# Two layers of attention and quantised feed-forward on one core: the passage from the first layer to the second put in another order

## The chip, the cores and the metric

One core of a Trainium2 chip runs the whole program once. The time is that of one execution on the device in microseconds; lower is better. Five instruction streams run side by side and wait for each other by semaphores: TensorE (PE), VectorE (DVE), ScalarE (ACT), GpSimd (POOL) and SyncE (SP, which here only issues transfers).

## What is computed

The input x is 8 batches of 256 rows of 512 values (16 row tiles of 128, `NT`; 8 batches, `NB`), with a context of 256 rows per batch. Two layers follow; each adds an attention and then a feed-forward part to x, both on a normalised x. Cut to what the change touches:

```python
# layer 0, feed-forward
h = square(relu(bitlinear(x, w1)))           # activations to 8 bits, weights to -1, 0, 1
x = x + bitlinear(h, w2)                     # "the way down"
# layer 1, cross-attention
Q = layernorm(x) @ W_qkv[:512].T             # projection
scores = coef * Q @ ctx.T                    # 256 scores for each row
thr = top_k(scores, 54)[-1]                  # the 54th largest
att = softmax(where(scores < thr, -inf, scores))
x = x + (att @ ctx) @ W_o.T                  # values, output projection
# layer 1, feed-forward
h = rms_norm(silu(bit_linear(x, w_gate)) * bit_linear(x, w_up), ln_weight)
x = x + bit_linear(h, w_down)
```

## The kernel before

Layer 0's attention, layer 0's feed-forward (`ffn0`) and layer 1 (`layer1`) are written one after another on every engine. Each part has a program per engine, a list of calls in an order written out by hand; there is no scheduler. A helper such as `pe_xb` is TensorE's share of a step, `act_qT` ScalarE's, and so on; each starts with the waits (`wait_ge`) that its inputs and its buffers need.

`ffn0` goes over the 16 row tiles. For tile n: transposes of the quantised row tile (`pe_x_turn`), the way up into the four banks of `quad` (`pe_up`, L1356), relu (L1453) and square (L1443) on ACT, rounding on DVE (`dve_hh`, L1578), transposes of the hidden values (`pe_h_turn`, L1370), their cast on ACT (`act_hT`, L1461), the way down (`pe_down`, L1381) and the residual on DVE (`dve_x2`, L1584), which SP stores to `x2_scratch`. Between these steps it also prepares layer 1's feed-forward weights in 48 chunks (`act_l`, L2575 and L2577, and the clip `dve_l`, L2582). The chunks 42 to 47 are finished in or after the passage to layer 1.

`layer1` handles a batch b (row tiles 2b and 2b+1) in stages s. In stage s batch s gets its projection and its scores, batch s-1 its weights, values and output projection, and the tiles of batch s-2 their feed-forward. The attention's matmuls run in float32 split in two parts (three products each, `PRODUCTS`), so each cast on ACT is followed by a subtraction on DVE or POOL that makes the lower part. The steps, by name and line:

- `pe_xa_turn` (L1779), `act_xT` (L2000), `dve_xT` (L2166): the normalised row tile is transposed and split. `dve_xa` (L2151 and three small ones) and `pool_xn` (L2401) make it.
- `pe_xb` (L1799), `act_qT` (L2006), `dve_qT` (L2172): projection, in two halves j of 24 matmuls.
- `act_ctx` and `pool_ctx` (L1990 and L1994 on ACT, L2390 on POOL): the context split for the scores (c = 0) and for the values (c = 1). `act_w`, `pool_w`: the same for the two attention weights.
- `pe_xc` (L1813), `act_sc` (L2014), `act_exp` (L2023): scores of a tile, 12 matmuls, their copy and exponential.
- `dve_top` (L2193) and six times `dve_round` (L2203, L2206): the search, 8 values of each row a round for both tiles of a batch. `dve_pm` (L2214) masks.
- `pe_xd` (L1828), `act_pT`, `dve_pT` (L2177): transposes of the attention weights.
- `pe_xe` (L1844), `act_oT`, `dve_oT` (L2183): values. `pe_xf` (L1859), `dve_x3` (L2188): output projection and residual.
- `dve_fa`, `pool_fn`, `dve_fq` (L2231), `act_xh` (L2038), `pe_x_turn` (L1877), `act_xq` (L2044): the tile normalised, quantised, transposed.
- `pe_gate_up` (L1892), `act_silu` (L2051), `dve_h` (L2247), `pool_hw` (L2433), `pe_h_turn`, `pe_down` (L1919), `dve_x4`: the feed-forward. Rounds of a search are put between the four `dve_h` of a tile.

PSUM has eight banks: `bA` (two), `bM`, `bT` and the four of `quad`. In layer 1 before the change the projection, scores, values and output projection use `bA[0]` and `bA[1]`, all float transposes `bT`, and only the feed-forward `quad`. `bA[1]` is also the bank of `ffn0`'s way down, so the second half of the first projection waits for the last residual:

```python
if b == 0:
    pe.wait_ge(f["w_lo"], 18)
    if j:
        pe.wait_ge(f["x2"], NT)
```

`pe_keep` issues matmuls on constants whose result nobody reads, ahead of a wait.

## Time and profile before

| | us |
|---|---|
| median of 3 runs | 1565.17 (1564.62 to 1567.32) |
| the profiled execution | 1567.12 |
| its span on the core | 1565.8 |
| TensorE busy | 1499.0 (96%) |
| VectorE busy | 1133.5 (72%) |
| ScalarE busy | 990.5 (63%) |
| GpSimd busy | 693.5 (44%) |

The span runs from the first to the last instruction; the execution's time has a little around it. Busy times are sums over instructions, and since matmuls overlap, a full TensorE need not be at its peak. The granted clock of TensorE over the span is 0.995 of full speed. Layer 0's attention lasts until about 870 us, its feed-forward until about 1195, and layer 1 has its regular turns from about 1265 on.

### The profile page before, as it was taken

Reading aid. Unit: us, or ns where it says so; the run is one execution under the profiler, and the core shown is the slowest. Engines: PE = TensorE matmul, PEld = TensorE weight load, DVE = VectorE, ACT = ScalarE, POOL = GpSimd, SP = SyncE. Lnnn points to the kernel's source line nnn. Section 1 sums busy time; section 2 is a strip of 40 time slices with the busy share of each in tenths; the row PEclk is TensorE's granted clock in tenths of the full one; section 3 lists DMA queues with packets and bytes.
Section 4 is the critical chain, followed back from the end, with each engine's and each line's share of the span. In section 5 each row is a group of like instructions: output and inputs, shape, how many; then the busy total and the mean of one; then the engine's idle time right before and its main releaser. Section 6 shows DMA issues by size and latency. Waiting matters only on the chain.

```text
span 1565.8 us, 26657 instructions
## 1 busy us (share of the span) xinstructions
PE 1499.0 (96%) x8840; PEld 1174.1 (75%) x8882; DVE 1133.5 (72%) x2966; ACT 990.5 (63%) x2502; POOL 693.5 (44%) x832
## 2 busy tenths in 40 slices
PE   7999999999999999999999899999996899999988
PEld 5778888888888888888887666666665666666653
DVE  7787777777777767777787745555556888888774
ACT  5666666666666666666677765666666576666655
POOL 5555555554555555555576200000005455555444
PEclk9999999999999999999999999999999899999999
DMA  7011111111111111111336666666655201111000
GB/s 277 28 54 55 41 68 41 48 62 41 49 61 41 60 46 40 60 47 48 122 124 265 242 243 215 219 220 220 222 183 190 80 21 55 55 48 41 28 14 28
DMA packets 50537, 156.73 MB, mean 100 GB/s; under 512 B 5600, under 2 KB 5728, under 8 KB 48992
## 3 DMA queue, kind: packets, MB, share of 16 engines
q1 hardware_dynamic: 50400, 155.02, 27.9%
q8 instruction: 72, 1.18, 0.3%
q14 instruction: 65, 0.53, 0.1%
HBM read 113.05 MB, written 41.94 MB: 99 GB/s over the span
## 4 chain that ended last, share of the span: by engine, by line
PE 75%; DVE 13%; ACT 5%; issue 3%; DMA 2%; POOL 2%; SPq 0%; ACTq 0%; DVEq 0%; POOLq 0%
PE bank L1327 11%; PE bank L368 10%; PE bank L421 9%; PE bank L338 8%; PE quad L408 5%; PE quad L1892 4%; PE bank L1381 3%; PE quad L1356 3%; PE bank L1919 3%; PE quad L396 3%; PE quad L398 3%; PE quad L397 3%; PE bank L1799 2%; PE bank L380 2%; PE bank L1859 1%
## 5 line engine op out<-in xcount | busy, mean ns | idle before, releaser
L617 ACT ACTIVATE Pt<-Pt,small 128x384 f32<-128x384 f32 (+1 forms) x256 | 172.8, 683 | 106.0 <-DVE small L877 105.9
L421 PE MATMUL bank<-PT,vv 128*128 128x512 f32 x672 | 200.2, 406 | 10.5 <-DVE PT L862 5.5
L368 PE MATMUL bank<-wq,xT 128*128 128x512 f32 x768 | 206.8, 404 | 1.3 <-DVE wq L772 0.8
L1137 POOL TENSOR_SCALAR Pt<-Pt,small 128x384 f32<-128x384 f32 (+1 forms) x256 | 164.7, 657 | 82.9 <-DVE small L885 82.8
L877 DVE CUSTOM_DVE_ANT_0 Pt<-quad,mask,small 128x384 f32<-128x384 f32 (+1 forms) x256 | 171.6, 679 | 33.8 <-PE quad L398 32.4
L1327 PE MATMUL bank<-wq,ot 128*128 128x512 f32 x768 | 189.2, 399 | 0.9 <-DVE xr L1513 0.8
L862 DVE TENSOR_TENSOR PT<-quad,PT 128x512 fp32r<-128x512 f32 x224 | 153.7, 686 | 38.5 <-ACT PT L609 38.1
L1327 PEld LDWEIGHTS bank<-wq,ot 128*128 128x128 f32 x768 | 142.7, 189 | 32.8 <-issue 1.2
L368 PEld LDWEIGHTS bank<-wq,xT 128*128 128x128 f32 x768 | 136.7, 188 | 26.9 <-DVE wq L772 2.1
L1125 POOL TENSOR_TENSOR t<-t 128x512 f32<-128x512 f32 x64 | 83.8, 1309 | 144.2 <-DVE t L843 144.2
L421 PEld LDWEIGHTS bank<-PT,vv 128*128 128x128 f32 x672 | 116.7, 189 | 34.8 <-DVE PT L862 12.8
L1630 POOL TENSOR_TENSOR cl<-cl,fixed 128x1 f32<-128x1 f32 x16 | 8.8, 551 | 297.8 <-DVE cl L1519 297.8
L609 ACT CAST PT<-quad 128x512 fp32r<-128x512 f32 x224 | 128.9, 591 | 7.0 <-PE quad L408 7.0
L408 PE MATMUL quad<-fixed,Pt 128*128 128x128 f32 x896 | 129.0, 272 | 0.9 <-POOL Pt L1137 0.9
L408 PEld LDWEIGHTS quad<-fixed,Pt 128*128 128x128 f32 x896 | 109.2, 140 | 24.4 <-POOL Pt L1137 2.2
L625 ACT CAST OT<-bank 128x512 fp32r<-128x512 f32 x64 | 37.6, 588 | 140.5 <-PE bank L421 140.5
L2433 POOL TENSOR_TENSOR bhw<-bh,lnw 128x512 f32<-128x512 f32 x64 | 81.7, 1276 | 82.8 <-DVE bh L2247 82.8
L396 PE MATMUL quad<-kT,qT 128*128 128x384 f32 (+1 forms) x256 | 99.4, 388 | 2.2 <-DVE small L877 0.8
L1131 POOL TENSOR_TENSOR small<-small,fixed 128x4 f32<-128x4 f32 x64 | 66.2, 1034 | 72.2 <-DVE small L849 72.1
L338 PE MATMUL bank<-wkc,cT 128*128 128x256 f32 x744 | 97.1, 287 | 0.6 <-issue 0.6
L338 PEld LDWEIGHTS bank<-wkc,cT 128*128 128x128 f32 x744 | 90.9, 191 | 8.2 <-DVE vv L828 7.0
L338 PE MATMUL bank<-wkv,xT 128*128 128x256 f32 x744 | 96.5, 286 | 0.0
(278 smaller groups left out, 3541.6 us busy)
## 6 DMA issues: line engine op xcount, KB each, us to landing
ot_scratch<-OT SPq DMA_DIRECT2D x64, 512.0 KB, 2.6
ot<-ot_scratch SPq DMA_DIRECT2D x64, 512.0 KB, 3.4
wkv_f<-in_w SPq DMA_DIRECT2D x12, 512.0 KB, 6.0
wkc_f<-in_w SPq DMA_DIRECT2D x12, 512.0 KB, 6.5
wkv_f<-in_wg SPq DMA_DIRECT2D x11, 512.0 KB, 4.3
wkv_f<-in_wd SPq DMA_DIRECT2D x11, 512.0 KB, 5.1
wkv_f<-in_wu SPq DMA_DIRECT2D x10, 512.0 KB, 4.9
stg<-in_ctxT SPq DMA_DIRECT2D x16, 256.0 KB, 3.5
```

The source lines that it names most:

```text
L338: ins = pe.matmul(kv_bank(u)[:, t * 256:t * 256 + 256], src[i][:, k, t * 128:t * 128 + 128], w[j][:, g, k, :], start=(n == 0), stop=(n == 11))
L368: ins = pe.matmul(bQ[:], xT[p][:, k, qt * 128:qt * 128 + 128], wq[j][:, g, k, :], start=(part == 0 and k == 0), stop=(part == 2 and k == 3))
L396: pe.matmul(bank[:, 0:n], qh, kh, start=True, stop=False)
L408: ins = pe.transpose(bP[k % 2][:, h * 128:h * 128 + 128], Pt[i % 2][:, h, kt * 128:kt * 128 + 128], idf[:])
L421: ins = pe.matmul(bO[:], vv[x][:, bg % 2, kt, :], PT[y][:, k % 2, :], start=(kt == 0 and n == 0), stop=(kt == tiles_in(i) - 1 and n == 2))
L609: act.copy(PT[0][:, k % 2, :], bP[k % 2]).then_inc(f["pt_hi"], 1)
L617: act.activation(p, p, ACT.Exp, bias=nm[:, i % 2, h:h + 1], scale=-1.0, accum_out=sm[:, i % 2, h:h + 1]).then_inc(f["s_exp"], 1)
L862: dve.tensor_tensor(PT[1][:, k % 2, :], bP[k % 2], PT[0][:, k % 2, :].bitcast(F32), ALU.subtract).then_inc(f["pt_lo"], 1)
L877: dve.tensor_tensor_reduce(Pt[i % 2][:, h, 0:n], bS[h % 2][:, 0:n], mask[:, 512 - n:512], scale=cq[:, i % 2, h:h + 1], scalar=3.0e38, op0= ...
L1125: pool.tensor_tensor(t1[:], t1[:], t2[:], ALU.add).then_inc(f["q_add"], 1)
L1137: pool.tensor_scalar(p, p, ri[:, i % 2, h:h + 1], 1.0, ALU.mult, ALU.mult).then_inc(f["p_n"], 1)
L1327: ins = pe.matmul(bY[:], ot[:, c % 4, i, k * 128:k * 128 + 128].bitcast(F32R), wo[j][:, g, k, :], start=(g == 0 and k == 0 and q == 0), st ...
```

## The change

The passage from `ffn0` to `layer1` is written in another order on every engine; what is computed stays the same, apart from `pe_keep` matmuls (5, 4 and 8 new ones; the 17 write banks that nobody reads at that time).

- Banks: new helpers choose the bank by batch or tile. The second half of batch 0's projection goes to `quad` bank 0, the scores of tiles 1, 2 and 3 to `quad` banks 0 and 1, the transposes of tiles 2 to 5 to `quad` banks 2 and 3.
- TensorE: `ffn0` ends its last tile with `pe_first`. There batch 0's projection is done in one piece, its scores come behind the transposes of the hidden values, and the last way down comes behind the scores and the transposes of batch 1. Batch 1's projection and scores follow. Stage 1 then goes from weights and values straight to the output projection, with the transposes of tiles 4 and 5 between.
- ACT and DVE: `act_first`, `dve_first` and `dve_second` write out stage 0 and stage 1 for these engines. The chunks 42 to 44 come behind batch 1's projection on ACT, 45 to 47 behind the first casts for batch 2. The last residual (`dve_x2`) stands behind the first round of batch 0's search. Batch 1's search has four rounds ahead of the first `dve_h`, before three.
- POOL: batch 1's context parts come ahead of the output weights. SP: three loads of context come earlier, ahead of the last store and the norm weights.

```diff
+    def q_bank(b, j):
+        return quad[:, 0, :] if (b, j) == (0, 1) else bA[j][:]
+
+    def s_bank(n):
+        return quad[:, n % 2, :] if n in (1, 2, 3) else bA[n % 2][:]
+
+    def x_bank(n):
+        return quad[:, 2 + n % 2, :] if 2 <= n < 6 else bT[:]
...
             if j:
-                pe.wait_ge(f["x2"], NT)
+                pe.wait_ge(f["relu"], 6 * (NT - 1) + 1)
         if b == 1:
             pe.wait_ge(f["sc"], j + 1)
+            if j:
+                pe.wait_ge(f["x2"], NT)
...
+    def pe_first():
+        pe_xb(0, 0)
+        pe_xb(0, 1)
+        ffn["pe_h_turn"](NT - 1)
+        pe_xc(0)
+        pe_xc(1)
+        pe_xa_turn(2)
+        pe_xa_turn(3)
+        ffn["pe_down"](NT - 1)
+        pe_xb(1, 0)
+        pe_xb(1, 1)
+        mem["pe_keep"](bM[:], 5)
+        pe_xc(2)
+        pe_xc(3)
+        mem["pe_keep"](bM[:], 4)
...
             if n == NT - 1:
-                l1["act_qT"](0, 0)
+                l1["act_ctx"](0, 0)
...
+    def act_first():
+        act_xT(2)
+        act_xT(3)
+        for n in range(2):
+            act_sc(n)
+        for n in range(2):
+            act_exp(n)
+        act_ctx(1, 0)
+        act_w(2)
+        act_w(3)
+        act_qT(1, 0)
+        act_ctx(0, 1)
+        act_qT(1, 1)
+        for k in (42, 43, 44):
+            ffn["act_l"](k)
...
+    def dve_first():
+        dve_qT(0, 0)
+        dve_xa(2)
+        dve_qT(0, 1)
+        dve_xa(3)
+        dve_xT(2)
+        dve_top(0)
+        dve_xT(3)
+        dve_top(1)
+        dve_round(0, 0)
+        ffn["dve_x2"](NT - 1)
+        dve_round(0, 1)
+        dve_round(0, 2)
+        dve_qT(1, 0)
+        dve_round(0, 3)
+        dve_qT(1, 1)
+        dve_round(0, 4)
+        dve_round(0, 5)
+        dve_pm(0)
+        dve_xa(4)
+
+    def dve_second():
+
+        dve_top(2)
+        dve_top(3)
+        dve_xa(5)
+        dve_oT(0, 0)
+        dve_oT(0, 1)
+        for k in (42, 43, 44):
             ffn["dve_l"](k)
+        dve_xT(4)
+        dve_xT(5)
+        dve_x3(0)
+        dve_fa(0)
+        dve_round(1, 0)
+        dve_x3(1)
+        dve_fq(0)
+        dve_fa(1)
+        dve_round(1, 1)
+        for k in (45, 46, 47):
+            ffn["dve_l"](k)
+        for r in (2, 3):
+            dve_round(1, r)
```

How TensorE's instructions stand, from batch 0's projection to the transposes of its attention weights. `axT` and `aq` are the projection's operands, `hh` the hidden values, `bank<-wkv_h,wkc_h` and `bank<-wkc_h` the last way down, `akT`, `aqT` those of the scores, `axn` the normalised rows, `pm` the attention weights. Before:

```order
L1799 MATMUL bank<-axT,aq 128x256 x24
L1370 MATMUL bank<-idh,hh 128x128 x16
L1381 MATMUL bank<-wkv_h,wkc_h 128x512 x4
L1799 MATMUL bank<-axT,aq 128x256 x24
L1813 MATMUL bank<-akT,aqT 128x256 x24
L1779 MATMUL bank<-fixed,axn 128x128 x8
L1799 MATMUL bank<-axT,aq 128x256 x36
L1828 MATMUL bank<-fixed,pm 128x128 x4
```

And in the change:

```order
L1824 MATMUL bank<-axT,aq 128x256 x24
L1824 MATMUL quad<-axT,aq 128x256 x24
L1372 MATMUL bank<-idh,hh 128x128 x16
L1840 MATMUL bank<-akT,aqT 128x256 x12
L1840 MATMUL quad<-akT,aqT 128x256 x12
L1802 MATMUL quad<-fixed,axn 128x128 x8
L1383 MATMUL bank<-wkv_h,wkc_h 128x512 x4
L1824 MATMUL bank<-axT,aq 128x256 x48
L2696 MATMUL bank<-ones 128x512 x5
L1840 MATMUL quad<-akT,aqT 128x256 x24
L2696 MATMUL bank<-ones 128x512 x4
L1855 MATMUL bank<-fixed,pm 128x128 x4
```

The second half of the projection and the scores have moved ahead of the way down (one of its four rows is shown), and batch 1's scores (x24) ahead of the transposes of the weights.

TensorE again, from batch 0's values (`apT`, `avv`) to the first gate product. Before:

```order
L1844 MATMUL bank<-apT,avv 128x256 x24
L1779 MATMUL bank<-fixed,axn 128x128 x4
L1813 MATMUL bank<-akT,aqT 128x256 x24
L1859 MATMUL bank<-ao,aoT 128x512 x12
L1779 MATMUL bank<-fixed,axn 128x128 x4
L1859 MATMUL bank<-ao,aoT 128x512 x12
L1877 MATMUL bank<-idh,bxh 128x128 x4
L1892 MATMUL quad<-wg,bxq 128x512 x4
```

And in the change:

```order
L1871 MATMUL bank<-apT,avv 128x256 x24
L1802 MATMUL quad<-fixed,axn 128x128 x8
L1886 MATMUL bank<-ao,aoT 128x512 x24
L2696 MATMUL bank<-ones 128x512 x8
L1904 MATMUL bank<-idh,bxh 128x128 x4
L1921 MATMUL quad<-wg,bxq 128x512 x4
```

Batch 1's scores are gone from here, and nothing but transposes stands between values and output projection (`ao`, `aoT`).

ACT, from the last relu of layer 0 (`r<-quad`) to the exponential of batch 0's scores (`pm<-sc`). Before:

```order
L1453 ACTIVATE r<-quad 128x512 x2
L1443 ACTIVATE r<-r,cl 128x1024 x2
L2006 CAST aqT<-bank 128x512
L1461 ACTIVATE wkc_h<-bank 128x1024 x2
L1990 CAST akT<-cn 128x4x128 x2
L2575 ACTIVATE wkv_f<-wkv_f,small 128x1024
L2577 ACTIVATE wkc_h<-wkv_f 128x1024
L2575 ACTIVATE wkc_f<-wkc_f,small 128x1024
L2577 ACTIVATE wkc_h<-wkc_f 128x1024
L1979 CAST ao<-ao_in 128x1024 x2
L2014 ACTIVATE sc<-bank,fixed 128x256 x2
L2023 ACTIVATE pm<-sc,bcl 128x256 x2
```

And in the change:

```order
L1456 ACTIVATE r<-quad 128x512 x2
L2032 CAST akT<-cn 128x4x128 x2
L1446 ACTIVATE r<-r,cl 128x1024 x2
L2048 CAST aqT<-bank 128x512
L2048 CAST aqT<-quad 128x512
L1464 ACTIVATE wkc_h<-bank 128x1024 x2
L2042 CAST axT<-quad 128x4x128 x2
L2056 ACTIVATE sc<-bank,fixed 128x256
L2056 ACTIVATE sc<-quad,fixed 128x256
L2065 ACTIVATE pm<-sc,bcl 128x256 x2
```

The weight chunks 42 and 43 and the output weights (`ao`) have gone from this stretch, the context's casts have come ahead of the squares, and the casts for batch 1 (`axT`) stand ahead of the score copies.

## Rows read from the trace of the kernel before

**Rows 1.** Busy time by stretch; columns: stretch, length, then each engine, PEclk, DMA share, GB/s.
```profile
1200.00:1220.00 20.00, 13.95 (x90) 12.94 (x91) 16.19 (x57) 14.74 (x22) 11.81 (x10) 0.83 0.76 272
```

**Rows 2.** Timeline of PE (TensorE) between the layers; start, length, instructions, idle before.
```profile
1200.82 3.14 PE L1813 MATMUL bank<-akT,aqT 128*128 128x256 f32 x24 [1.40 <-DVE aqT L2172]
...
1207.44 0.83 PE L1779 MATMUL bank<-fixed,axn 128*128 128x128 f32 x4 [3.04 <-DVE axT L2166]
...
1209.74 6.67 PE L1799 MATMUL bank<-axT,aq 128*128 128x256 f32 x36 [1.47 <-DVE axT L2166]
...
1219.21 3.48 PE L1844 MATMUL bank<-apT,avv 128*128 128x256 f32 x24 [0.27 <-DVE apT L2177]
...
1226.46 3.01 PE L1859 MATMUL bank<-ao,aoT 128*128 128x512 f32 x12 [0.46 <-ACT sc L2014]
...
1235.54 0.61 PE L1877 MATMUL bank<-idh,bxh 128*128 128x128 f16 x4 [2.87 <-ACT bxh L2038]
...
1237.24 1.49 PE L1892 MATMUL quad<-wg,bxq 128*128 128x512 bf16 x3 [1.09 <-ACT bxq L2044]
...
1250.76 0.66 PE L1828 MATMUL bank<-fixed,pm 128*128 128x128 f32 x4 [1.50 <-DVE pm L2214]
```

**Rows 3.** Timeline of DVE (VectorE) between the layers.
```profile
1198.25 0.69 DVE L2151 BATCH_NORM_STATS2 bcl<-xs_a 128x6 f32<-128x512 f32 x1
...
1200.07 0.69 DVE L2172 TENSOR_TENSOR aqT<-bank,aqT 128x512 fp32r<-128x512 f32 x1 [0.67 <-ACT aqT L2006]
...
1205.10 0.41 DVE L2203 MATCH_REPLACE8 wk<-bcl,sc 128x256 f32<-128x256 f32 x1
...
1211.17 0.09 DVE L2203 MATCH_VALUE_LOAD wk<-bcl,wk 128x8 f32 x1
...
1212.75 0.09 DVE L2203 MATCH_VALUE_LOAD wk<-bcl,wk 128x8 f32 x1
...
1215.90 0.48 DVE L2214 SCALAR_TENSOR_TENSOR pm<-sc,bcl,pm 128x256 f32<-128x256 f32 x1
...
1225.03 0.89 DVE L2582 TENSOR_SCALAR wkc_h<-wkc_h 128x1024 bf16<-128x1024 bf16 x2
...
1240.92 0.75 DVE L2247 SCALAR_TENSOR_TENSOR bh<-quad,bcl,sg 128x512 f32<-128x512 f32 x1 [0.52 <-ACT sg L2051]
...
1250.63 0.74 DVE L2247 SCALAR_TENSOR_TENSOR bh<-quad,bcl,sg 128x512 f32<-128x512 f32 x1
```

**Rows 4.** Timeline of PE, two neighbouring turns of layer 1's loop.
```profile
1302.39 1.67 PE L1813 MATMUL bank<-akT,aqT 128*128 128x256 f32 x12 [0.44 <-DVE aoT L2183]
...
1344.84 1.66 PE L1813 MATMUL bank<-akT,aqT 128*128 128x256 f32 x12 [0.45 <-DVE aoT L2183]
```

**Rows 5.** Timeline of ACT (ScalarE) between the layers.
```profile
1187.93 2.19 ACT L1443 ACTIVATE r<-r,cl 128x1024 f32<-128x1024 f32 x2 [0.48 <-DVE cl L1568]
...
1192.48 1.13 ACT L1990 CAST akT<-cn 128x512 fp32r<-128x512 f32 x2
...
1202.56 0.47 ACT L2014 ACTIVATE sc<-bank,fixed 128x256 f32<-128x256 f32 x1 [0.63 <-PE bank L1813]
...
1209.83 1.15 ACT L2575 ACTIVATE wkv_f<-wkv_f,small 128x1024 f32<-128x1024 f32 x1
...
1211.97 1.13 ACT L2575 ACTIVATE wkv_f<-wkv_f,small 128x1024 f32<-128x1024 f32 x1
...
1234.76 0.72 ACT L2038 ACTIVATE bxh<-fn,bcl 128x512 f16<-128x512 f32 x1 [4.24 <-DVE bcl L2239]
```

**Rows 6.** Timeline of POOL (GpSimd), same stretch.
```profile
1209.49 2.52 POOL L2390 TENSOR_TENSOR avv<-cn,avv 128x512 fp32r<-128x512 f32 x2 [1.51 <-ACT avv L1994]
```

**Rows 7.** Longest waits of SP's DMA queue: line, waited for, total, times, longest.
```profile
SPq L1753 <- DMA x_scratch<-xr: 3.9, 1, 3.9
```

**Rows 8.** DMA issues from 1199 to 1210: KB each, us from issue to landing.
```profile
xs_a<-x_scratch SPq DMA_DIRECT2D x2, 256.0 KB, 5.2
```

**Rows 9.** PE alone by stretch: length, PE busy, PEclk, DMA share, GB/s.
```profile
1210.00:1215.00 5.00, 5.00 (x26) 0.55 0.62 200
```

More of the change, by code:

```diff
@@ L1808, in pe_xc @@
         pe.wait_ge(f["cx_lo0"], 2 * b + 2)
-        after(pe, f["ao_lo"], 2 * (b - 1) + t + 1 if b else 0)
+        after(pe, f["ao_lo"], 2 * (b - 1) + t + 1 if b > 1 else 0)
+        if n == 1:
+            pe.wait_ge(f["relu"], 6 * (NT - 1) + 2)
         i = 0
@@ L1889, in pe_gate_up @@
             after(pe, f["h_j"], 4 * n + j - 1)
+            if n == 0 and j == 1:
+                pe.wait_ge(f["xat_lo"], 6)
             for w, o in ((wg, 0), (wu, 1)):
@@ L1949, in pe_program @@
                 pe_x_turn(n + 1)
-            if s + 1 < NB and s:
+            if s + 1 < NB:
                 pe_xa_turn(2 * s + 2)
-            if x_:
+            if s == 1:
+                pe_xa_turn(5)
+            if x_ and s != 1:
                 pe_xc(2 * s)
                 pe_xc(2 * s + 1)
-            if s == 0:
-                pe_xa_turn(2)
             if s == NB:
@@ L1960, in pe_program @@
                 pe_xf(2 * o)
-            if s + 1 < NB:
+            if s + 1 < NB and s != 1:
                 pe_xa_turn(2 * s + 3)
@@ L2091, in act_gate_up @@
         act_square(n, 3)
+    def act_first():
[13 more added lines that the diff above has]
+            ffn["act_l"](k)
     def act_program():
-        for s in range(NB + 3):
+        act_first()
+        for s in range(1, NB + 3):
             x_, o_, f_, g_ = stages(s)
@@ L2102, in act_program @@
                 act_hT(n - 1, 1)
-            if s == 1:
-                act_qT(s, 0)
             if o_:
                 act_pT(o)
-            if x_:
+            if x_ and s != 1:
                 act_qT(s, 1)
+            if s == 1:
+                for m in (2, 3):
+                    act_sc(m)
+                for m in (2, 3):
+                    act_exp(m)
             if o_:
@@ L2125, in act_program @@
                 act_levels(n)
-            if s:
+            if s != 1:
                 act_ctx(s, 1)
-            else:
-                act_xT(2)
-            if x_:
+            if x_ and s != 1:
                 act_exp(2 * s)
                 act_exp(2 * s + 1)
-            if s + 1 < NB:
+            if s + 1 < NB and s != 1:
                 act_xT(2 * s + 3)
-            if s == 0:
-                act_ctx(s, 1)
-                for k in (44, 45, 46):
-                    ffn["act_l"](k)
             if f_:
@@ L2297, in dve_gate_up @@
                 dve_hmax(n, 0)
-    def dve_last(s, part):
-        first, end = {(1, 0): (44, 46), (1, 1): (46, 48)}.get((s, part), (0, 0))
-        for k in range(first, end):
-            ffn["dve_l"](k)
+    def dve_first():
[25 more added lines that the diff above has]
+        for k in (42, 43, 44):
+            ffn["dve_l"](k)
+        dve_xT(4)
[7 more added lines that the diff above has]
+        dve_round(1, 1)
+        for k in (45, 46, 47):
+            ffn["dve_l"](k)
+        for r in (2, 3):
+            dve_round(1, r)
     def dve_program():
-        for s in range(NB + 3):
+        dve_first()
+        for s in range(1, NB + 3):
             x_, o_, f_, g_ = stages(s)
             o, n = s - 1, 2 * (s - 2)
-            left = [(o, r) for r in range(2 if s == 1 else 3, 6)] if o_ else []
+            left = [(o, r) for r in range(4 if s == 2 else 3, 6)] if o_ and s > 1 else []
             if f_:
                 dve_gate_up(n, left, s if x_ else None, None, o if o_ else None)
-            elif o_:
-                for b, r in left:
-                    dve_round(b, r)
-                dve_pm(o)
             if g_:
                 dve_x4(n - 1)
-            if s == 1:
-                dve_qT(s, 0)
             if o_:
@@ L2322, in dve_program @@
                 dve_ri(o)
[L2323 to L2359 removed]
+            if s == 1:
+                dve_second()
+            else:
+                if s + 1 < NB:
+                    dve_xa(2 * s + 2)
+                if x_:
+                    dve_qT(s, 1)
+                if f_:
+                    dve_f_var(n)
+                if o_:
+                    dve_oT(o, 0)
+                if f_:
+                    dve_fc(n)
+                if o_:
+                    dve_oT(o, 1)
+                if s + 1 < NB:
+                    dve_xa(2 * s + 3)
+                if x_:
+                    dve_top(2 * s)
+                    dve_top(2 * s + 1)
+                if s + 1 < NB:
+                    dve_xT(2 * s + 2)
+                if o_:
+                    dve_x3(2 * o)
+                    dve_fa(2 * o)
+                if s + 1 < NB:
+                    dve_xT(2 * s + 3)
+                if o_:
+                    dve_x3(2 * o + 1)
+                    dve_fq(2 * o)
             if f_:
```

121 lines of the change are left out of this document (47 added, 74 removed).

## The prediction

> **What bounds the kernel now.** I read the busy times by stretch first, then TensorE's timeline, then those of the engines it waits for. Over the span TensorE is the full engine. Between the layers it is not: from 1200 to 1220 it is busy 13.95 of 20 us and its granted clock falls to a mean of 0.83 [rows 1]. Its timeline shows holes there of 1.40, 3.04, 1.47, 0.46, 2.87, 1.09 and 1.50 us [rows 2]; each names VectorE (DVE) or ScalarE (ACT). So the transition is a chain through all engines, and DVE's search for the 54th largest score is its core: rounds of 1.58 us (1211.17 to 1212.75), six per batch, the first at 1205.0, done when the masking starts at 1215.90 [rows 3]. After it layer 1 runs in turns 42.45 us apart with TensorE idle 0.45 us at most in the row shown [rows 4]. A turn has no fixed time in it that I can find, so what the transition gains or loses, the end should gain or lose: **the question is how much earlier the first regular turn starts.** I follow the chain to the last of DVE's four products of gate and up for tile 0 (L2247, at 1250.63) and to TensorE's transposes of batch 1's weights at 1250.76.
>
> **The change, step by step.** Times are those of the profiled execution; both orders are the same up to the first projection of batch 0 at 1185.7.
>
> *Scores of batch 0.* ACT gets two casts of the context (1.13 us) ahead of the two squares, where it now starts at 1187.93 after an idle 0.48 [rows 5]. Net delay 0.6: squares done at 1190.7, second rounding on DVE at 1191.4. The other half of the projection, 24 matmuls (about 3.1 us, the 24 score matmuls of the same width take 3.14 [rows 2]), goes to a quad bank and so no longer waits for the last way down; it runs inside TensorE's wait for that rounding and ends at 1191.9. ACT casts both halves (0.57 each, half of the 1.13 in [rows 5]), the second till 1192.5; DVE does its subtraction (0.69) and one row tile's statistics (about 1.15: 0.69 and three small ones [rows 3]) and its second subtraction by 1193.8. The scores can start at 1193.85 instead of 1200.82: **7.0 us early**. The other score operand is ready: POOL needs 2.5 us [rows 6] from 1188.
>
> *First round.* Scores 3.14, then the first transposes of batch 1 (about 0.4), then on ACT two casts (1.1) ahead of two score copies (0.47 each [rows 5]), then a subtraction and a maximum on DVE (1.1): first round at 1200.5 against 1205.0, **4.5 early**; putting transposes and casts ahead costs 2.5 of the 7.0. The last way down (16 matmuls, 3.4) lies behind the transposes and beside ACT's casts, at 1197.6 to 1201.0, and is free.
>
> *The search.* Six rounds as before (9.5). Before, two subtractions and a 0.26 wait lay among them; now the last residual (0.75) and two subtractions (0.7 each). Masking starts at 1211.95 against 1215.90: **3.95 early**. Batch 1's whole projection (6 us) and its scores (3.1) sit on TensorE from 1201.0 to 1211.9 beside the rounds, at no cost: the rounds cover them. ACT's list there (two casts of context 1.1, two of the output weights 2.0, a projection half 0.6, two of values 1.1, the other half, then three weight chunks at 2.14 each, from 1209.83 to 1211.97 [rows 5]) ends at 1214.0.
>
> *Values.* Transposes of the weights at 1212.95 to 1213.4; ACT comes free 0.6 later, casts to 1214.6, DVE subtracts to 1215.3. First value matmul 1215.35 against 1219.21 [rows 2]: **3.9 early**. DVE's statistics of row tile 4 lie inside that wait.
>
> *Output projection.* Now batch 1's transposes and scores, a late score copy (0.46 idle) and another cast lie between values and projection: 7.25 us from 1219.21 to 1226.46 [rows 2]. In the change only 3.0 of values, two sets of transposes (0.4 each) and some 0.4 of waiting for the second normalised tile, whose statistics DVE ends at 1217.6 and POOL uses until 1219.0. ACT and DVE have both halves ready at 1219.7. Start 1219.8: **6.7 early**. From there to the first gate product the chain is the same (residual, statistics, POOL's normalisation, quantising, cast, transposes): 10.78 now [rows 2], so 1230.55 against 1237.24. The one search round put in between runs while POOL normalises.
>
> *To the regular turn.* DVE then has one set of statistics (1.15), a round, three clips (0.89 for two, so 1.2 [rows 3]) and two rounds: 7.0 us from 1228.05. Now it is statistics, three rounds and a 0.52 wait for the first sigmoid product: 6.2 from 1234.7 to 1240.92 [rows 3, 5]. First product 1235.0: 5.9 early. Inside the four products there is now one round fewer (four rounds done ahead, not three) and no 0.23 wait: 1240.92 to 1250.63 is 9.7, so 7.95. Last product 1242.95 against 1250.63: **7.7 us early**.
>
> The sum: the profiled execution took 1567.12 (span 1565.8 and 1.3 around it); less 7.7 that is 1559.4 (span 1558.1). The median of the runs, 1565.17, lies 1.95 below that execution, so **1557.5**. The seventeen filler matmuls (5, 4, 8) stand before waits; if all of them were in the way, they would cost 3.7 at 0.215 each (my estimate from 3.0 us for 12 float matmuls of the same width, which take a little more), if none, 0. I take 0: in my sum each batch ends before what TensorE waits for, the last by 1.8.
>
> **What the chain does not show.** The masking reads two SBUF tensors and takes 0.48 at 1215.90 [rows 3], when POOL's value parts (2.52 from 1209.49 [rows 6]) are over. In the change POOL does context parts, output weights and value parts one after another to 1211.3, and the masking comes at 1211.95, 0.65 later. The Trainium skill (SBUF — State Buffer, section "SBUF: two separate sides") says that a VectorE operation with two SBUF inputs and a GpSimd operation take the shared port pair in turn, the loser blocked for the whole of the other. By that rule an overlap would hold the masking for up to one value part, 1.26 us, and the gain would be 6.4; no row here shows an overlap, and by my times there is none.
>
> **Rivals.**
>
> *1. Half of it is lost on late loads or on a falling clock.* The row store waits for the residual, now at 1202.85 (before 1196.2). SP then waits 3.9 us for the store [rows 7] before it issues the norm weights and rows 4 and 5, which take 5.2 to land [rows 8]: 1213.3, while DVE asks for both at 1212.85 and has slack to about 1213.5 before the values wait. Every us later costs one us. For the clock: it is near 0.5 from 1210 to 1215 [rows 9], after holes of 3.04 and 1.47 with one group of transposes between them, and again at 1237.24 after 2.87 and 1.09; it does not fall after a single 1.40 or 1.50 with full work around it [rows 2]. The change leaves holes of 1.2, 0.9, 1.95 and 0.4, each between full work, and 1.8 plus 1.45 before the gate product, where a fall is hidden as it largely is now, since DVE's rounds come last. A fall at the 1.95 would cost the values 3.0. Result 1559 to 1562.3.
>
> *2. No change.* A gain of the transition that a later turn takes back. For it: a wait that only shows once the turns start earlier (a transfer, a buffer) can't be excluded. Against: the turns repeat to 0.02 us [rows 4], so they start when their inputs do. 1564 to 1566.5.
>
> *3. Slower: TensorE at its 1.2 GHz level through the chain.* Place: the hole before the scores at 1192.7, then values and projection. Price: scores +3.0, values +3.0, output projection +5.5 (24 matmuls at 3.01 per 12 [rows 2]), together 11.5, so 1569. It beats the gain once values and projection both run at the lower level (8.5). For it: 36 matmuls took 6.67 where 24 take 3.14 [rows 2]. Against: the lower stretches now last some 5 us and need holes twice as long as those left.
>
> **Numbers.** The forecast has 62%, rival 1 24%, rival 2 7%, rival 3 7%. The measurement can tell 0.2%, 3.1 us. Forecast and rival 1 both lie below 1562.0: faster 0.86, same 0.07, slower 0.07. The forecast's own spread is 1555.5 to 1559.5 (waits between engines that I set near zero against fillers and clock); reaching into rival 1 gives 1555.3 to 1562.6.
>
> **What would show it.** Right: TensorE's scores of batch 0 at about 1194, first round near 1200.5, masking near 1212, values near 1215.4, output projection near 1220, gate product near 1230.5, last product near 1243, and turns still 42.4 apart. Wrong: DVE waiting for rows 4 and 5 (a DMA named before its statistics), a granted clock near 0.5 between 1214 and 1226, TensorE idle before the output projection for more than 1 us, or DVE's last product later than 1247 with the end moved by as much.

## The result, and the profile after

The change brings 3.0 us, not 7.7. The median of 20 runs is 1563.99 us (1561.82 to 1566.77) against 1567.57 us (1564.62 to 1569.81) in 20 runs of the kernel before; ratio 0.9981, 95% interval 0.9975 to 0.9988, which is 1.9 to 3.9 us. The two medians lie 3.6 us apart, inside the same interval; the text counts by the ratio. The profiled execution has a span of 1561.2 us against 1565.8.

Both kernels vary by 5 us from execution to execution, and in the profiles most of that lies ahead of the passage: the first projection of batch 0 starts at 1185.72 in the profile before, at 1183.88 in the one after, and at 1184.0 to 1188.0 in those of the runs below. So every time here is taken from that projection ("+33.5"). TensorE after:

```profile
1192.21 1.69 PE L1840 MATMUL bank<-akT,aqT 128*128 128x256 f32 x12 [1.44 <-DVE aqT L2230]
...
1213.69 4.64 PE L1871 MATMUL bank<-apT,avv 128*128 128x256 f32 x24 [1.72 <-DVE apT L2235]
...
1219.74 5.73 PE L1886 MATMUL bank<-ao,aoT 128*128 128x512 f32 x24 [0.53 <-DVE aoT L2241]
...
1230.37 0.81 PE L1921 MATMUL quad<-wg,bxq 128*128 128x512 bf16 x3 [0.92 <-ACT bxq L2086]
...
1246.10 0.66 PE L1855 MATMUL bank<-fixed,pm 128*128 128x128 f32 x4 [2.74 <-DVE pm L2272]
```

Set beside [rows 2 and 3]:

| step, from the first projection | before | after | gain | predicted |
|---|---|---|---|---|
| scores of batch 0 | +15.1 | +8.3 | 6.8 | 7.0 |
| masking of batch 0 | +30.2 | +26.5 | 3.7 | 3.95 |
| values | +33.5 | +29.8 | 3.7 | 3.9 |
| output projection | +40.7 | +35.9 | 4.9 | 6.7 |
| first product of gate and up | +55.2 | +53.3 | 1.9 | 5.9 |
| transposes of batch 1's weights | +65.0 | +62.2 | 2.8 | 7.7 |

Up to the values the sum holds to 0.25 us. Then it loses at three places. The first is inside the values: their 24 matmuls take 4.64 us where [rows 2] have 3.48 and the prediction reckoned 3.0, at a granted clock that by stretch (start, length, PE busy, PEclk, DMA share, GB/s) reads

```profile
1214.00:1219.00 5.00, 5.00 (x32) 0.66 0.71 249
```

The other two are on VectorE. Its timeline after:

```profile
1187.71 2.18 DVE L1581 TENSOR_SCALAR hh<-r 128x1024 f16<-128x1024 f32 x2 [1.34 <-ACT r L1446]
...
1210.36 0.48 DVE L2272 SCALAR_TENSOR_TENSOR pm<-sc,bcl,pm 128x256 f32<-128x256 f32 x1
...
1211.18 0.69 DVE L2209 BATCH_NORM_STATS2 bcl<-xs_a 128x6 f32<-128x512 f32 x1
...
1230.80 1.55 DVE L2669 TENSOR_SCALAR wkv_h<-wkv_h 128x1024 bf16<-128x1024 bf16 x1
1232.27 1.82 DVE L2669 TENSOR_SCALAR wkc_h<-wkc_h 128x1024 bf16<-128x1024 bf16 x2
...
1237.15 0.75 DVE L2305 SCALAR_TENSOR_TENSOR bh<-quad,bcl,sg 128x512 f32<-128x512 f32 x1
...
1244.16 0.48 DVE L2272 SCALAR_TENSOR_TENSOR pm<-sc,bcl,pm 128x256 f32<-128x256 f32 x1
...
1244.56 1.48 DVE L2272 SCALAR_TENSOR_TENSOR pm<-sc,bcl,pm 128x256 f32<-128x256 f32 x1
```

The three clips of chunks 45 to 47 take 3.3 us where 1.2 were reckoned, and batch 1's second mask 1.48 where the first takes 0.48. Neither row has a wait in brackets: VectorE had its semaphores and the instruction itself was long. What GpSimd did at those times:

```profile
1186.19 2.55 POOL L2474 TENSOR_TENSOR akT<-cn,akT 128x512 fp32r<-128x512 f32 x2 [2.72 <-ACT akT L2032]
...
1230.78 2.68 POOL L2474 TENSOR_TENSOR avv<-cn,avv 128x512 fp32r<-128x512 f32 x2
...
1244.32 1.43 POOL L2517 TENSOR_TENSOR bhw<-bh,lnw 128x512 f32<-128x512 f32 x1 [1.56 <-DVE bh L2305]
```

A product of GpSimd had begun 0.02 us before the first long clip and 0.24 us before the long mask. The same shows without any timeline, in the groups of VectorE's instructions by line and form (count, busy time, mean ns). Before:

```profile
L1578 DVE TENSOR_SCALAR hh<-r 128x1024 f16<-128x1024 f32 x32 | 22.2, 694 | 20.2 <-ACT r L1443 20.2
L2214 DVE SCALAR_TENSOR_TENSOR pm<-sc,bcl,pm 128x256 f32<-128x256 f32 x16 | 7.1, 482 | 0.3
L2582 DVE TENSOR_SCALAR wkc_h<-wkc_h 128x1024 bf16<-128x1024 bf16 x10 | 4.0, 421 | 1.8 <-ACT wkc_h L2577 1.7
L2582 DVE TENSOR_SCALAR wkv_h<-wkv_h 128x1024 bf16<-128x1024 bf16 x7 | 2.8, 418 | 0.1
```

And after:

```profile
L1581 DVE TENSOR_SCALAR hh<-r 128x1024 f16<-128x1024 f32 x32 | 23.0, 722 | 20.2 <-ACT r L1446 20.2
L2272 DVE SCALAR_TENSOR_TENSOR pm<-sc,bcl,pm 128x256 f32<-128x256 f32 x16 | 8.1, 544 | 0.3
L2669 DVE TENSOR_SCALAR wkc_h<-wkc_h 128x1024 bf16<-128x1024 bf16 x10 | 4.9, 526 | 0.3 <-ACT wkc_h L2664 0.3
L2669 DVE TENSOR_SCALAR wkv_h<-wkv_h 128x1024 bf16<-128x1024 bf16 x7 | 4.1, 580 | 0.1
```

The same instructions in the same number cost 1.0 us more for the masks, 2.2 for the clips (0.9 and 1.3) and 0.8 for the roundings of hidden values. Theory A: GpSimd's products hold these VectorE instructions. Its rivals: they wait for something else (B), or TensorE's clock alone took the 4.9 us (C).

For theory A the kernel before has a hint that the prediction passed over. GpSimd there:

```profile
1221.08 1.10 POOL L2401 TENSOR_SCALAR axn<-xs_a,bcl 128x512 f32<-128x512 f32 x1
1225.20 0.76 POOL L2393 TENSOR_TENSOR bcl<-bcl,fixed 128x1 f32<-128x1 f32 x1 [3.02 <-DVE bcl L2156]
```

Both begin while VectorE has a clip under way (two clips from 1220.86, and the pair at 1225.03 of [rows 3]), and both are long: elsewhere in this stretch the same two instructions take 0.77 and 0.55.

### The profile page after: what moved, and what is told of

Read it like the earlier page. It is cut to its first block and busy times, and to the rows that moved or that the text cites. A ratio compares the mean times of both kernels' runs of the same rounds, so it can differ in the third digit from the quotient of the medians.

```text
span 1561.2 us, 26693 instructions
## 1 busy us (share of the span) xinstructions
PE 1497.2 (96%) x8857; PEld 1173.9 (75%) x8899; DVE 1137.1 (73%) x2966; ACT 989.5 (63%) x2502; POOL 692.4 (44%) x832
```

## The experiments

Each kernel is the change with one edit, unless said otherwise, and each ratio is against the kernel before.

**1. Batch 1's value parts wait for the last clip.**

```diff
                 pool_fn(2 * o + 1)
+                pool.wait_ge(f["w_ter"], 40)
                 pool_ctx(s, 1)
```

> One wait more on GpSimd: batch 1's two value parts begin only when the last weight clip (chunk 47) is through; nothing else moves. Theory A (while GpSimd's two value parts run, VectorE's clips are held): in the change the three clips took 1.55 and 1.82 us (3.2 in all) beside them, the three before them, with GpSimd idle, 0.75 for two and 0.42. Here the three take 1.2 in all, the value parts run beside two search rounds and these stay at 1.57 each, ACT's first silu starts by some 1.9 us earlier, the first gate-and-up product stands at about +51.3 us behind the first projection instead of +53.3, the last one, held by the mask alone, at about +60.2, and the time is 1.8 to 2.1 us below the change's: about 4.9 us under the kernel before, ratio 0.9969. Theory B (the clips wait for ACT's chunks or for their turn and only look long): still 3.2 in all, time as the change, ratio 0.9981. Theory C (the lost 4.9 us are all TensorE's clock): clips may get shorter, the time stays at 0.9981.

Ratio 0.9964 (0.9951 to 0.9976). VectorE:

```profile
1231.41 0.43 DVE L2670 TENSOR_SCALAR wkv_h<-wkv_h 128x1024 bf16<-128x1024 bf16 x1
1231.76 0.76 DVE L2670 TENSOR_SCALAR wkc_h<-wkc_h 128x1024 bf16<-128x1024 bf16 x2
...
1232.89 0.41 DVE L2261 MATCH_REPLACE8 wk<-bcl,wk 128x256 f32<-128x256 f32 x1
1233.22 0.74 DVE L2264 MAX8 bcl<-wk 128x8 f32<-128x256 f32 x2
```

and GpSimd's value parts now beside the search rounds:

```profile
1232.60 2.52 POOL L2474 TENSOR_TENSOR avv<-cn,avv 128x512 fp32r<-128x512 f32 x2 [1.16 <-DVE wkc_h L2670]
```

The clips take 1.2 us and the rounds keep their 0.41 and 0.74. The first gate-and-up product comes at +49.6. In this execution the values also took only 3.14, with nothing changed ahead of them; experiment 4 takes that up. So the execution to compare it with is the repetition of the change there, whose values are as fast: its first product comes at +51.8. The 2.2 us between the two are the clips, at an equal clock, and B and C fall for them.

**2. GpSimd's third norm-weight product waits for the masks.**

```diff
+            if n == 0 and j == 2:
+                pool.wait_ge(f["pm"], 4)
```

> One wait more on GpSimd: the third norm-weight product of row tile 0 begins only when both masks of batch 1 are written. Theory A (a VectorE instruction with two SBUF inputs is held while a GpSimd product runs): the second mask takes 0.48 us instead of 1.48, the last gate-and-up product comes 1.0 us earlier, TensorE's transposes of batch 1's weights stand at +61.2 instead of +62.2 us behind the first projection, the time falls by 0.9 to 1.0: ratio about 0.9975. GpSimd's delayed product ends at about 1246.3 where the next one starts at 1246.8, so nothing is paid for the wait. Theory B (the mask waits for something else, its exponential or ACT): 1.48 stays, 0.9981. Theory D (the wait holds GpSimd's norm weights, and through them the tile's maximum and levels): the mask is short but the time is not below the change's, 0.9981 or above.

Ratio 0.9971 (0.9960 to 0.9981). VectorE's masks of batch 1:

```profile
1246.82 0.47 DVE L2272 SCALAR_TENSOR_TENSOR pm<-sc,bcl,pm 128x256 f32<-128x256 f32 x1
...
1247.22 0.48 DVE L2272 SCALAR_TENSOR_TENSOR pm<-sc,bcl,pm 128x256 f32<-128x256 f32 x1
```

1.48 has become 0.48, and the transposes of batch 1's weights come 7.96 us after the first product of gate and up instead of 8.95. Theory A holds here too. Theory D falls by the profile, in which the rest of the span is as long as before (315.03 against 315.04); the time itself, 0.9971 with an upper bound of 0.9981, does not tell this kernel from the change.

**3. The value parts in pieces.** Experiment 1 shows that GpSimd's work is the cause, not how it holds. Here each of the two instructions is cut into four of 128 columns, which still run beside the clips:

```diff
+            if b == 1 and c:
+                for q in range(3):
+                    u = slice(q * 128, q * 128 + 128)
+                    pool.tensor_tensor(lo[:, u], src[:, u], hi[:, u].bitcast(F32), ALU.subtract)
+                lo, hi, src = lo[:, 384:512], hi[:, 384:512], src[:, 384:512]
```

> Batch 1's value parts on GpSimd in pieces of 128 columns, four for each of the two, instead of one instruction of 512; they still run beside the three weight clips. If a clip is held until the GpSimd instruction then running is through (Theory A in its strict form), what it waits for is one small piece: the first clip takes 0.8 to 0.9 us instead of 1.55, the second and third about the same or less, the three 2.0 to 2.6 in place of 3.2, and the time falls by 0.6 to 1.2 below the change: ratio near 0.9975. If a clip is held until all of GpSimd's work is through, or shares its access in small turns: 3.2 as before. If it waits for nothing of GpSimd's, 3.2 as well, but the run with the wait has excluded that.

Ratio 0.9974 (0.9963 to 0.9984). VectorE, then GpSimd:

```profile
1230.90 0.73 DVE L2674 TENSOR_SCALAR wkv_h<-wkv_h 128x1024 bf16<-128x1024 bf16 x1
1231.55 1.27 DVE L2674 TENSOR_SCALAR wkc_h<-wkc_h 128x1024 bf16<-128x1024 bf16 x2
```

```profile
1230.89 1.65 POOL L2477 TENSOR_TENSOR avv<-cn,avv 128x128 fp32r<-128x128 f32 x3
1232.50 0.63 POOL L2479 TENSOR_TENSOR avv<-cn,avv 128x128 fp32r<-128x128 f32 x1
1233.10 1.29 POOL L2477 TENSOR_TENSOR avv<-cn,avv 128x128 fp32r<-128x128 f32 x3
1234.35 0.46 POOL L2479 TENSOR_TENSOR avv<-cn,avv 128x128 fp32r<-128x128 f32 x1
```

The first clip is held for 0.3 us instead of 1.1, in proportion to the GpSimd instruction that had begun before it: one piece takes 0.43 alone (1.29 for three), a whole part 1.3. The three clips take 1.9, a little less than the 2.0 to 2.6 expected, and the first gate-and-up product comes at +51.9 where the change's first profile, with values as slow, has +53.3. GpSimd is held in turn: its four pieces beside the clips take 2.2 us, the next four, beside a search round, 1.7. So each side waits for the instruction of the other that is under way. That is what the Trainium skill says (SBUF — State Buffer, section "SBUF: two separate sides"): the port pair is locked for a whole instruction, and whoever comes second is fully blocked. It names the VectorE instructions that ask for the pair: those with two SBUF inputs, as the mask, and those in a 2-port mode; that the clip and the rounding belong to the latter agrees with these rows. The search's instructions, which read one wide SBUF operand, are unaffected in experiment 1 (0.41 and 0.74 beside a value part).

**4. The change again, and the hole before the values filled.** The repetition has no edit; the other kernel has

```diff
                 pe_xd(o)
+            if s == 1:
+                mem["pe_keep"](bM[:], 7)
```

> The change as it is, once more, for the question whether the slow value matmuls (4.64 us for 24 in its first profile, 3.14 in those of the two runs with one wait more, which are the same up to there) belong to the change or to one execution. If to one execution: values 3.14, output projection at +34.35 us behind the first projection, transposes of batch 1's weights at +60.75, and a ratio of 0.9973 (0.9963 to 0.9983, for the 4.3 us that the passage is shorter then). If to the change: values again some 4.6, transposes at +62.2, 0.9981.

> Seven filler matmuls more on TensorE, between the transposes of batch 0's weights and its values, where the change has a hole of 1.72 us. Theory C (the granted clock falls after that hole, and that is what the values lost): the 24 value matmuls take 3.1 to 3.3 us instead of 4.64, the output projection starts at about +34.4 us instead of +35.9 behind the first projection, the granted clock of the 20 us from 1200 is 1.0 instead of 0.91, and the time falls by 1.2 to 1.5: ratio 0.9972. Rival (the values are slow for a reason of their own, an operand that comes late or a bank in use): 4.6 us as before, 0.9981, or slower by up to 0.3 where the fillers end behind the operand. If the gain of the values is lost again before the regular turns, the values are short and the time is unchanged: then the search of batch 1, not TensorE, sets the end.

Ratios 0.9973 (0.9963 to 0.9983) and 0.9979 (0.9970 to 0.9989). TensorE in the repetition:

```profile
1215.07 3.13 PE L1871 MATMUL bank<-apT,avv 128*128 128x256 f32 x24 [1.73 <-DVE apT L2235]
...
1245.96 1.11 PE L1855 MATMUL bank<-fixed,pm 128*128 128x128 f32 x4 [2.73 <-DVE pm L2272]
1246.73 4.02 PE L1824 MATMUL bank<-axT,aq 128*128 128x256 f32 x24
```

and with the fillers:

```profile
1214.95 3.15 PE L1871 MATMUL bank<-apT,avv 128*128 128x256 f32 x24 [0.20 <-DVE apT L2237]
...
1245.88 0.66 PE L1855 MATMUL bank<-fixed,pm 128*128 128x128 f32 x4 [2.73 <-DVE pm L2274]
1246.29 3.12 PE L1824 MATMUL bank<-axT,aq 128*128 128x256 f32 x24
```

The slow values belong to single executions: behind the same hole of 1.72 us they took 4.6 in three profiles (the change's first, experiment 3, and experiment 5, whose fillers ahead of it are gone) and 3.14 in four (the repetition, experiments 1, 2 and 7). The repetition shows a second place. Behind the hole of 2.73 us before the weights' transposes, which the kernel before has as 1.50 [rows 2], the granted clock is at half (0.50 from 1246 to 1248, the level of 1.2 GHz), the projection half takes 4.02 instead of 3.12 (4.0 to 4.6 in the four profiles that show this), and the turn that follows lasts 43.76 us instead of 42.5. Eight profiles have this hole; four of them (the repetition, experiments 3, 6 and 7) have a first turn of 43.8 to 44.0, the others 42.5. The repetition expected one of two outcomes and got values that were fast and a loss elsewhere, which neither had named. With the fillers the hole is 0.20 us long and the values take 3.15, but they take no longer in four profiles with the hole, and the time is not to be told from the change's: that the fillers prevent the fall is not shown by this run alone.

**5. Without the 17 fillers.** The three calls with 5, 4 and 8 are taken out of the change.

> The change without its 17 filler matmuls (5 ahead of batch 1's scores, 4 ahead of the weights' transposes, 8 ahead of the first transposes of the feed-forward). The prediction gave them no cost and no part in the gain. By that: every step at the same place, ratio as the change's, 0.9973 to 0.9981. If they hold the clock: TensorE is idle for 2.1 us before batch 1's scores, 1.0 more before the transposes and 3.7 before the feed-forward's, the granted clock is near 0.5 for the values and perhaps the output projection, the values take 4.6 to 6.1 us, and the time is 1.5 to 3 above the change's: ratio 0.9985 to 1.0000. If they are in the way: 0.3 to 1 us faster than the change, 0.997.

Ratio 0.9986 (0.9977 to 0.9995), 2.2 us. The output projection stands at +35.87, the first gate-and-up product at +53.28 and the weights' transposes at +62.23: to 0.01 us as in the change's first profile, so the fillers stand in nobody's way, as predicted. The granted clock is 0.50 from 1228 to 1233 and the first gate product 0.4 us late, but the search hides it. Whether the fillers save a fall in some executions is open: the interval overlaps the change's.

**6. The last way down ahead of batch 0's scores again.**

```diff
         ffn["pe_h_turn"](NT - 1)
+        ffn["pe_down"](NT - 1)
         pe_xc(0)
...
         pe_xa_turn(3)
-        ffn["pe_down"](NT - 1)
```

> One part undone: the first layer's last way down stands ahead of batch 0's scores again, on TensorE alone; the bank of the second projection half, the order of the other engines and batch 1's scores stay as in the change. The prediction's chain (scores, search, values and projection follow one another without slack): the way down runs from about +8.5 to +12.1 us behind the first projection, the scores start at +12.1 instead of +8.3, everything behind them is 3.7 us later, the transposes of batch 1's weights at +64.5 where the change has +60.8 with an unbroken clock, and the ratio is 0.9997 (0.9988 to 1.0005): most of the change's gain gone. Rival (the gain came from batch 1's scores leaving the place between values and output projection, and the start of the search has slack): +61 and 0.9975.

Ratio 1.0000 (0.9991 to 1.0009). TensorE:

```profile
1193.64 0.81 PE L1383 MATMUL bank<-wkv_h,wkc_h 128*128 128x512 bf16 x3 [1.00 <-ACT wkc_h L1464]
...
1196.68 1.77 PE L1840 MATMUL bank<-akT,aqT 128*128 128x256 f32 x12
```

The scores come at +10.9, 2.6 us later and not 3.7: the way down starts at +7.9, 0.4 before the scores would have, and takes 3.0 (1193.64 to 1196.68); the delay is still 2.4 at the weights' transposes (+63.1). So there is no slack in the search, and of the 4.3 us by which the change's passage is shorter with an unbroken clock, 2.4 come from this one exchange. Where the other 1.9 come from (batch 1's scores taken out from between values and output projection is the candidate) no run separates. The first turn was slow in this profile (44.0), which takes 1.6 of the 1.9 back; in how many of the runs it is so is not known.

**7. The second context part waits for the roundings.**

```diff
+            if b == 0 and c == 0 and t == 1:
+                pool.wait_ge(f["hh"], 2 * NT)
```

> The change with one wait more on GpSimd: the second context part of batch 0 begins only when both roundings of the last hidden values are through. In the change these roundings took 2.18 us for two beside GpSimd's context parts, in the kernel before 0.69 each with GpSimd idle. Theory A (GpSimd's product holds the rounding): 1.3 for the two, TensorE's transposes of the hidden values 0.8 us earlier; the scores start 0.3 to 0.8 us earlier, at +7.5 to +8.0 behind the first projection instead of +8.34, since GpSimd's part ends later, at about +6.5, and ACT's second cast is not earlier; everything behind them moves by as much, transposes of batch 1's weights at about +60.2 instead of +60.7, ratio 0.9970. If the scores wait for ACT's cast and not for VectorE: roundings short, scores at +8.3, time as the change's, 0.9973 to 0.9981.

Ratio 0.9975 (0.9966 to 0.9984). VectorE:

```profile
1190.46 0.69 DVE L1581 TENSOR_SCALAR hh<-r 128x1024 f16<-128x1024 f32 x1 [1.34 <-ACT r L1446]
1191.51 0.69 DVE L1581 TENSOR_SCALAR hh<-r 128x1024 f16<-128x1024 f32 x1 [0.35 <-ACT r L1446]
```

The roundings are short, the scores start at +7.89 instead of +8.34, and all that follows is 0.4 earlier (transposes at +60.3). A third kind of instruction is held by GpSimd, at a place where half of the 0.8 us was hidden behind ACT (the bracket of 0.35). In this execution, too, the first turn was slow.

**8. Both waits and the filled hole together** (edits 1, 2 and the fillers of 4).

> The three edits together: value parts behind the last clip, third norm-weight product behind the masks, seven fillers ahead of the values. If the three losses lie one behind another on the chain, their sizes add up: 1.9 + 1.0 + 1.3 = 4.2 us below the change, 7.2 us below the kernel before, ratio 0.9954, and the weights' transposes of batch 1 at about +58.0 us behind the first projection instead of +62.2. If one hides another (the rounds of batch 1's search begin at a time set by the output projection, so that the clock's part may be swallowed), 2.9 to 3.5 below the change: 0.9958 to 0.9963. If the three are not the cause, 0.9981.

Ratio 0.9951 (0.9939 to 0.9964), 7.7 us. TensorE:

```profile
1216.47 3.13 PE L1871 MATMUL bank<-apT,avv 128*128 128x256 f32 x24 [0.21 <-DVE apT L2237]
...
1244.19 0.66 PE L1855 MATMUL bank<-fixed,pm 128*128 128x128 f32 x4 [1.73 <-DVE pm L2274]
```

The transposes stand at +57.5, 7.5 us ahead of the kernel before. The losses lay one behind another and none hid another; the short mask also makes the second hole 1.73 us long, and no slow turn followed it here or in experiment 2.

**9. Two moves more on VectorE, and the score copies first.** The first kernel takes the one of experiment 8 and puts a search round ahead of the first residual, each following round one place earlier, and the masks ahead of the third product:

```diff
-            if j == 3 and b_pm is not None:
+            if j == (2 if b_pm == 1 else 3) and b_pm is not None:
...
+        dve_round(1, 0)
         dve_x3(0)
```

> The kernel with the two waits and the seven fillers (transposes of batch 1's weights at +57.54 us behind the first projection), with two moves more on VectorE alone. The first round of batch 1's search stands ahead of the first residual, in VectorE's 0.95 us of waiting for the output projection, and the following ones move up; and both masks of batch 1 stand ahead of the third gate-and-up product instead of the fourth. If VectorE's work is what the end of the passage waits for: first gate-and-up product at +48.7 instead of +49.6, the weights' transposes 0.7 to 1.7 us earlier still than that alone, at about +55.9, time 1.6 us below the run with the three edits, ratio 0.9941. If TensorE or ACT now bounds (the residual stands 0.6 us later, and the feed-forward's first product with it): +57 and 0.9948 to 0.9951.

The second adds the wait of experiment 7 and

```diff
     def act_first():
-        act_xT(2)
-        act_xT(3)
         for n in range(2):
             act_sc(n)
+        act_xT(2)
+        act_xT(3)
...
-        pe_xc(3)
         mem["pe_keep"](bM[:], 4)
...
             if s == 1:
-                mem["pe_keep"](bM[:], 7)
+                pe_xc(3)
```

with the two maxima and the first round on VectorE ahead of the two subtractions in the same way, the last residual of layer 0 behind the second round, and chunk 44 in the later group.

> The same with the wait of the context part, with batch 0's score copies ahead of the casts for batch 1 on ACT (and the two maxima and the first round ahead of the two subtractions on VectorE), with chunk 44 moved to the group of 45 to 47, and with the scores of tile 3 in the place of the seven fillers, behind the transposes of batch 0's weights. VectorE waits 3.2 us before its first subtraction now; the maxima fill it. Expected if the search is still the chain: first round some 2.5 us earlier, masks of batch 0 1.3 to 1.6 earlier (VectorE's own work is 11.4 us from the first round to them, and takes two subtractions more in), output projection 1.3 earlier, transposes of batch 1's weights at about +54.5, ratio 0.993. If the fourth chunk in the later group delays ACT's first cast of the feed-forward (it has 2.0 us of slack and the chunk takes 2.13): +55.5 to +56, no gain over the run without.

Ratios 0.9950 (0.9935 to 0.9964) and 0.9937 (0.9922 to 0.9952). The first stands at +56.8 and not at +55.9: its first product waits 0.94 us for ACT, whose order now bounds the end, the case that the expectation had as its rival. By time it is not faster than experiment 8 (0.9950 against 0.9951). The second stands at +55.5:

```profile
1215.39 3.14 PE L1871 MATMUL bank<-apT,avv 128*128 128x256 f32 x24
...
1242.27 0.60 PE L1855 MATMUL bank<-fixed,pm 128*128 128x128 f32 x4
```

It starts from one that was 0.9 later than expected and gains 1.4, as expected (the wait for ACT is still 0.80). But +55.5 is also the near end of the expectation's other case, a fourth chunk that delays ACT's first cast of the feed-forward: ACT begins that cast without a break behind the chunk, 0.39 us after VectorE's last level begins where the first kernel has 0.17. How much of the gain each of its edits brings is not separated. At a median of 1558.6 us it is the fastest kernel of the study, 9.9 us below the kernel before (7.5 to 12.2).

**Do the profiles add up to the times?** For each kernel the passage (first projection to the transposes of batch 1's weights) and the rest of the span, less the same of before (65.04 and 315.04), against what the runs gave:

| kernel | passage | rest | by its profile | by its runs (95%) |
|---|---|---|---|---|
| the change | 62.22 | 315.10 | -2.8 | -3.0 (-3.9 to -1.9) |
| the change again | 60.72 | 316.44 | -2.9 | -4.2 (-5.8 to -2.7) |
| 1, value parts wait | 58.55 | 314.98 | -6.6 | -5.6 (-7.7 to -3.8) |
| 2, mask alone | 59.76 | 315.03 | -5.3 | -4.5 (-6.3 to -3.0) |
| 3, small pieces | 60.85 | 316.67 | -2.6 | -4.1 (-5.8 to -2.5) |
| 4, hole filled | 60.76 | 315.02 | -4.3 | -3.3 (-4.7 to -1.7) |
| 5, no fillers | 62.23 | 315.18 | -2.7 | -2.2 (-3.6 to -0.8) |
| 6, way down first | 63.11 | 316.65 | -0.3 | 0.0 (-1.4 to +1.4) |
| 7, context waits | 60.32 | 316.45 | -3.3 | -3.9 (-5.3 to -2.5) |
| 8, three edits | 57.54 | 315.11 | -7.4 | -7.7 (-9.6 to -5.6) |
| 9, first kernel | 56.83 | 315.44 | -7.8 | -7.8 (-10.2 to -5.6) |
| 9, second kernel | 55.48 | 315.23 | -9.4 | -9.9 (-12.2 to -7.5) |

They do: every profile's value lies inside the interval of its runs, experiment 3's close to its edge. The change's own 3.0 can be put together from the parts: 4.3 with an unbroken clock, less 1.5 in three of seven profiles at the first hole, less 1.4 in four of eight at the second: 4.3 - 0.65 - 0.7 = 2.95. The two shares come from seven and eight single profiles of different kernels, so this is an estimate, and that it meets 3.0 so closely is luck; the two timings of this one kernel gave 3.0 and 4.2.

## Why the prediction was wrong

**What held.** The chain and its head: scores 7.0 early (6.8), first round 4.5 (4.2), masks 3.95 (3.7), values 3.9 (3.7). The output projection's 6.7 and the first gate product's 6.7 hold wherever the clock does: in experiment 8 they are 6.4 and 6.7. That the turns pass the gain on holds as well, since the rest of the span is 315.0 to 315.2 in every profile whose first turn ran at full clock but one (315.4, the first kernel of experiment 9). The fillers cost nothing. With the collisions and the falls taken out, the sum of 7.7 is there: 7.5 in the profile, 7.7 by the runs.

**What failed: one step, "three clips (0.89 for two, so 1.2 [rows 3])".** The duration was taken from a row beside which GpSimd had only a product of one column (1225.20, 0.76 instead of 0.55: it was the clip that held GpSimd), and set down where, by the change's own order, GpSimd begins batch 1's value parts. They took 3.3. Price: 2.2 us at the end of the passage (experiment 1). In the next sentence of the sum, "9.7, so 7.95", the four products take 8.8, of which 1.0 is the held mask (experiment 2). The prediction had the rule in its hands and laid it beside one instruction, the masks of batch 0, where nothing overlaps, and said so rightly; its "no row here shows an overlap" is true of masks only, since the kernel before shows GpSimd held beside the clips at two places. The three places where something does overlap in the change were not looked through. One of them stands in the prediction's own times: GpSimd's context parts from 1188 for 2.5 us, and a rounding that ends at 1191.4. This hold costs 0.4 (experiment 7) and is among the small terms. The order of GpSimd's instructions beside VectorE's would have shown them.

**The clock.** Rival 1 had a fall at the hole before the values, priced at 3.0. It measured 1.5 (4.64 against 3.14), what about half of the 24 matmuls cost at the lower level, and it comes in some executions only. The hole before the transposes of batch 1's weights appears in no sentence. It is 2.73 us instead of 1.50, and 1.0 of that is again the held mask, since with the mask free it is 1.73 (experiments 2 and 8). A slow first turn behind it costs 1.3 to 1.6, in four of the eight profiles with 2.73 and in neither of the two with 1.73; two are too few to say that the short mask cures it. The prediction followed the chain up to that very instruction and took the turns behind it as fixed. Together the two falls are 1.35 us on the average, by the estimate above.

**The sum of it.** 2.2 for the clips, 1.0 for the mask, 1.35 for the clock and 0.2 of small terms (7.7 against the 7.5 of experiment 8): 4.75, which is 7.7 less 2.95. The clips and the mask are measured by an edit each; the clock's term is an estimate, and why it falls in some executions stays open.

**Late loads,** the other half of rival 1, did not happen: VectorE's statistics of row tile 4 (the row at 1211.18) wait for nothing. Rival 2, a gain taken back by a later turn, held only for the slow first turn. Rival 1 in its own terms (1559 to 1562.3, which is 2.9 to 6.2 below 1565.17) has the measured 3.0 at its edge, but more of the loss came from the hold, which it doesn't contain. Rival 3, a low clock from the scores through the output projection, did not happen: behind the slow values the projection's 24 matmuls took 5.73, less than twice the 3.01 for 12 [rows 2]. Of the signs of being wrong two came: a granted clock of 0.66 from 1214 to 1219, and VectorE's last product at +62.1, which on the clock of the profile before is 1247.8.

**The time itself.** 2.4 us of the distance between 1557.5 and 1563.99 are none of these: the kernel before gave 1565.17 in three runs and 1567.57 in twenty.

## What to carry to other kernels

A duration read from a row holds for what the other engines did during that row. When instructions change places, lay GpSimd's new order beside VectorE's and look at each VectorE instruction that has two SBUF inputs or is of the kind of the clip and the rounding (one input in SBUF, output in SBUF, 1024 columns in 0.42 and 0.69 us): beside a GpSimd product of 1.3 us it cost 1.0 to 1.1 here. One wait on GpSimd's side gave that back in full, GpSimd's work cut into quarters gave back 1.4 of the clips' 2.1. Comparing the groups by form before and after finds such a loss in a minute: the same instructions, the same count, more busy time, and no wait in brackets.

## What was not expected of the hardware

The hold goes both ways: a GpSimd product that begins in the middle of the first mask takes 1.43 us instead of 1.27 (1244.32 above), and the four pieces beside the clips 2.2 instead of 1.7.

Behind the same hole of 1.7 us TensorE's granted clock falls in some executions and not in others. The values were slow in the three profiles whose first projection starts at 1183.9 to 1184.1, and fast in the four with this hole that start it at 1185.2 or later. Whether that decides the fall was not tried. What makes an execution reach the passage up to 4 us earlier or later is in part the clock itself: the granted clock drops below 1 between 36 and 42 us and again between 874 and 882 in the profiles of experiments 1, 2, 7 and 8, which start the projection at 1186.0 to 1188.0, and at neither place in the three early ones. It is not all of it, since the first kernel of experiment 9 has neither drop and starts at 1187.3.
